# A wait for the landing behind each slot's four gathers in two layers of a graph network

## The reference

```
# layer 1 (graph attention, 4 heads)          # layer 3 (typed attention, 8 heads)
e = leaky_relu(a_s[src] + a_d[dst], 0.2)      attn = sum(Q[dst] * K[src]) * rel_scale[rel] / sqrt(16)
m = segment_max(e, dst)                       attn = attn - max(attn)
p = exp(e - m[dst])                           attn_exp = exp(attn)
z = segment_sum(p, dst)                       attn_sum = segment_sum(attn_exp, dst)
out = segment_sum(h[src]*p/z[dst], dst)       out = segment_sum(attn_exp/attn_sum[dst] * V[src], dst)
```

## Time and profile before

| | |
|---|---|
| time, median of 3 runs | 11803.96 us (11802.01 to 11812.33) |
| the profiled execution, its own time | 11689.37 us |
| its span | 11687.6 us |
| TensorE (PE) busy with matmuls / with weight loads | 6719.7 us (57%) / 5717.7 us (49%) |
| VectorE (DVE) busy | 4983.8 us (43%) |
| ScalarE (ACT) busy | 1831.9 us (16%) |
| GpSimd (POOL) busy | 6138.8 us (53%) |
| DMA over the span | 878.74 MB, mean 75 GB/s |

### The profile page before, as it was taken

How to read it: one execution, slowest core, us unless ns; L and a number is a source line. 1 busy time by engine, 2 the same in 40 slices (tenths; PEclk the granted TensorE clock), 3 DMA queues, 4 the chain that set the end, 5 groups by cost and what they waited for, 6 DMA issues and landing times. The chain is left out here.

```text
span 11687.6 us, 97629 instructions
## 1 busy us (share of the span) xinstructions
PE 6719.7 (57%) x31067; PEld 5717.7 (49%) x31067; DVE 4983.8 (43%) x11243; ACT 1831.9 (16%) x3088; POOL 6138.8 (53%) x6479
## 2 busy tenths in 40 slices
PE   4555555555436666666544545545543677777775
PEld 4444444444336666666534444444432455555553
DVE  4444444444552222222345555555555344444444
ACT  0000000000110000000110000000011454444543
POOL 4554555544216666666445555555530566666663
PEclk6666666666655555555566666666655677777776
DMA  4222222222112222222134343334320222222221
GB/s 133 73 76 75 76 76 73 76 76 76 36 28 55 55 56 54 55 55 55 50 122 122 120 124 120 122 120 122 122 68 1 65 63 61 61 61 61 63 61 38
DMA packets 388341, 878.74 MB, mean 75 GB/s; under 512 B 134341, under 2 KB 202872, under 8 KB 368224
## 3 DMA queue, kind: packets, MB, share of 16 engines
q0 software_dynamic: 232704, 536.56, 18.1%
q1 hardware_dynamic: 150242, 324.95, 8.5%
q10 hardware_dynamic: 4896, 11.01, 0.2%
HBM read 839.65 MB, written 32.40 MB: 75 GB/s over the span
## 5 line engine op out<-in xcount | busy, mean ns | idle before, releaser
L619 POOL DMA_INDIRECT PM<-gat_table,src_idx x1616 | 1525.6, 944 | 1532.7 <-PE ps L658 1023.2
L2074 POOL DMA_INDIRECT TMP<-schnet_table,src_idx x1616 | 1558.2, 964 | 1336.9 <-DVEq L2176 481.6
L1588 POOL DMA_INDIRECT PM<-hgt_kv_table,src_idx x1616 | 1527.7, 945 | 1356.8 <-PE ps L1620 743.2
L1148 POOL DMA_INDIRECT TMP<-gcn_table,src_idx x1616 | 1524.9, 944 | 1166.1 <-issue 452.9
L1166 PE MATMUL ps<-rows,PM 16*128 16x8 f32 x3232 | 756.1, 359 | 772.2 <-DVE PM L1213 755.3
L1166 PEld LDWEIGHTS ps<-rows,PM 16*128 16x128 f32 x3232 | 717.8, 323 | 871.5 <-DVE PM L1213 785.2
L1620 PE MATMUL ps<-PM 128*128 128x136 f32 x3232 | 628.0, 362 | 578.7 <-DVE PM L1709 577.6
L2101 PE MATMUL ps<-PM 128*128 128x128 f32 x3232 | 623.0, 355 | 488.9 <-issue 371.4
L1620 PEld LDWEIGHTS ps<-PM 128*128 128x128 f32 x3232 | 578.9, 261 | 612.7 <-DVE PM L1695 602.3
L1173 PE MATMUL ps<-TMP 128*128 128x128 f32 x3232 | 838.4, 441 | 0.2 <-DVE TMP L1207 0.2
L2101 PEld LDWEIGHTS ps<-PM 128*128 128x128 f32 x3232 | 572.1, 266 | 521.8 <-issue 521.4
(11 more groups left out here) (370 smaller groups left out, 9510.2 us busy)
## 6 DMA issues: line engine op xcount, KB each, us to landing
PM<-local_dst_row SPq DMA_DIRECT2D x101, 1024.0 KB
PM<-local_dst_row SPq DMA_DIRECT2D x202, 512.0 KB
PM<-in_attrT SPq DMA_DIRECT2D x101, 400.0 KB
PM<-gat_table,src_idx POOLq DMA_INDIRECT x1616
TMP<-gcn_table,src_idx POOLq DMA_INDIRECT x1616
PM<-hgt_kv_table,src_idx POOLq DMA_INDIRECT x1616
TMP<-schnet_table,src_idx POOLq DMA_INDIRECT x1616
xT<-in_rel_row SPq DMA_DIRECT2D x101, 128.0 KB
```

The lines of the kernel that those rows point to most:

```text
L619: pool.indirect_dma_start(out=g[:, par, t, 0:ROW0], out_offset=None, in_=tab0_d, in_offset=bass.IndirectOffsetOnAxis(ap=src_idx[:, i * ROU ...
L1148: pool.indirect_dma_start(out=g[:, b, k, :], out_offset=None, in_=tab1_d, in_offset=bass.IndirectOffsetOnAxis(ap=src_idx[:, (i * SLOTS + b ...
L1588: pool.indirect_dma_start(out=g[:, par, t, 0:2 * P], out_offset=None, in_=kv_d, in_offset=bass.IndirectOffsetOnAxis(ap=src_idx[:, i * ROUN ...
L2074: pool.indirect_dma_start(out=g[:, b, k, :], out_offset=None, in_=tab3_d, in_offset=bass.IndirectOffsetOnAxis(ap=src_idx[:, (i * SLOTS + b ...
```

## The change

One line is added in each of the two gather programs, behind the four gathers of a slot: GpSimd waits until that slot's gathers have all landed, and then goes on to the next slot. `g_ready[par][b]` is the semaphore that the gathers raise and that ScalarE (layer 1) and VectorE (layer 3) wait for as well; each gather adds 16, and slot `b` of half `par` is filled for the (j + 1)th time, so the value waited for is `16 * KT * (j + 1)`. The waits make 404 in each layer. All other instructions and their order on each engine stay as they were.

```
@@ layer 1 @@
                             t = b * KT + k
                             pool.indirect_dma_start(out=g[:, par, t, 0:ROW0], out_offset=None, in_=tab0_d,
                                                     in_offset=bass.IndirectOffsetOnAxis(ap=src_idx[:, i * ROUND + t:i * ROUND + t + 1], axis=0)).then_inc(g_ready[par][b], 16)
+                        pool.wait_ge(g_ready[par][b], 16 * KT * (j + 1))
                 straight(round_)
```

## The result

The change makes the kernel slightly slower: 11834.63 us (median of 11 runs, 11822.67 to 11848.08) against 11801.03 us before (11 runs, 11784.31 to 11813.63); ratio 1.0026, 95% interval 1.0018 to 1.0034. Forecast were 11464 us. The profiled execution has a span of 11832.9 us, 145 more than the one of before. The profile of before is of an execution of 11689 us, though, and the change was timed beside executions of 11801, so the differences between the two profiles need not add up to the difference of the times.

What follows compares the result with a forecast made beforehand. Bound: the VectorE/TensorE chain, delayed by TensorE completions seen late during gather bursts. Rounds of 29.9 and 27.1 us becoming 26.7 and 26.9 save 320 + 20 = 340 us: 11804 - 340 = 11464 us, range 11150 to 11830.

Steps and rivals of the forecast that it cites:

- The mechanism: Layers 1 and 3: rests behind each slot clear the gather backlog, so TensorE's completions come at once and GpSimd bounds.
- The chains: VectorE and TensorE steps of a round, claimed to need 19.7 us (layer 1) and 16.0 us (layer 3) without the delay.
- hold: TensorE's completions seen late by the waiting engine during gather bursts; put at 10.2 us a round (layer 1), 11.1 (layer 3).
- The second rival: Pauses too short: TensorE's completions stay held, bursts grow 4.4 us a round, 12684 us; slower outcomes had chance 0.20.
- the slots alone: Four slots a round, each 6.45 us including 2.45 for the landing: 25.8 us a round.
- the loads: SyncE's 1 MB a round falling beside an awaited gather: 0.9 us a round in layer 1, 1.1 in layer 3.
- one landing: Time from a slot's last gather start until its bytes are there and noticed: taken as 2.45 us.
- The prediction's sign for rests of 1.8 us with rounds over 28: What the changed profile would show if the VectorE and TensorE chains were longer than read.
- Only the third and fourth gather of a slot can pass their delay on: Reason for taking 0.9 us a round, from 0 to 3.7, for layer 1's load meeting a gather.
- The first rival: Layers cancel: shared DMA engines cost 2.7 us a round, rounds 28.5, layer 1 gains 140, layer 3 loses 140; chance 0.09.
- cost range of 24.8 to 31.8 us: Bounds of a round of four slots under the waits: landing seen with its bytes, or only when TensorE's completions are.
- The estimate worked out from "Anatomy of one DMA": About 2.0 us fixed plus bytes over 436 GB/s: a 70 KB gather lands in 2.2 us, a round takes 24.8.

Runs made afterwards that it cites:

- small_loads: The changed kernel, both waits kept, with SyncE's loads cut to 16 numbers a partition: 11402.27 us, ratio 0.9758 to the kernel before.
- the fourth set: Runs in which the kernel before took 9293.34 us; the change, run again there, took 11134.02 us, ratio 1.1987.
- pace_128: Kernel before plus GpSimd zeroing 128 numbers a partition behind each gather, no landing wait: ratio 0.9165 with the hold, 1.0711 without.
- pace_192: Kernel before plus GpSimd zeroing 192 numbers a partition behind each gather, no landing wait: 10811.37 us, ratio 0.9264.
- rest_long: Kernel before plus GpSimd zeroing a 128 x 512 scratch behind each slot's four gathers, no landing wait: 10990.79 us, ratio 0.9292.
- rest_640: Kernel before plus GpSimd zeroing 640 numbers a partition behind each slot, no landing wait: 10868.88 us, ratio 0.9295.

## Why the prediction was wrong

- **The mechanism held.** TensorE's completions come at once when GpSimd rests 1.8 us behind each slot, L807 and L816 lose their waits, and GpSimd becomes the bound. The chains fit under it with room: without hold and waits they fit under rounds of 20.0 us. The second rival (completions stay held, 12684) is refuted.
- **The step that failed is the size of a round under the waits.** Forecast were 26.7 and 26.9 us, measured 28.0 and 30.0, and with 29.8 and 27.1 before that turns a gain of 320 + 20 into a gain of 183 and a loss of 297 by the two profiles. By its terms (small_loads): the slots alone were put at 25.8 and take 26.4 and 27.9; the loads were put at 0.9 and 1.1 and cost 1.6 and 2.1. In layer 1 each term is short by 0.6 to 0.7 us, in layer 3 by 2.1 and 1.0. The largest error is that one landing, read off at 544 B a row in layer 1, was carried over to layer 3 at 1024 B. There, with small loads, two rests are 0.2 us longer than in layer 1, one 0.3 and one 0.9 (medians); the cause of the 0.9 stays open. The prediction's sign for rests of 1.8 us with rounds over 28 was longer chains, and it would have misled: the rounds are long because one or two rests in four are longer than 1.8 to 2.0.
- **"Only the third and fourth gather of a slot can pass their delay on"** was the argument for a small load term. It takes the meeting for chance. In the trace the load is issued during the same slot in 99 of 101 rounds of layer 1, and in layer 3 one of its halves during the first slot's last gather in 99 of 101, since by the code its cue (the four one-hot matrices) hangs on the chain that starts with a slot's landing. The trace of before could have said so: there the load of layer 1 comes behind a burst's last gather in 99 of 101 rounds. The first rival assumed the meeting and had the right sign for layer 3, but rounds of 28.5 in both layers, where 28.0 and 30.0 were measured; that its total of 11804 comes within 31 us of the result is luck.
- **The sum of the two layers** was the weak point of the whole: a large gain and a small one of opposite risk. Layer 3 had 0.2 us a round of forecast gain and a cost range of 24.8 to 31.8 us; a chance of loss there stood nowhere by itself.
- **The base of the sum** was mixed: rounds were read from an execution of 11689 us and their difference taken off a median of 11804. With the measured rounds the same sum gives 11804 - 183 + 297 = 11918, and 11834.63 was measured; so taking the rounds and the base from executions of two kinds would have put the sum off by some 80 us even with every round right.
- **The Trainium skill**, "DMA: Bandwidth & Descriptors", "Rules for kernel authors", says to issue early and wait late. The rule's sign was right for layer 3 and for the fourth set, and wrong for layer 1 where the hold exists, which gained 183 us. The estimate worked out from "Anatomy of one DMA" (24.8 us a round) was lower than mine and further off: the rows of small_loads give 26.4 and 27.9.
- **What no step had** is that the hold is not always there. Every figure of the earlier trace rows came from one execution; in the fourth set, where the hold is absent, the change costs 19.9%. The range, whose upper end of 11830 stood 5 us under the result, allowed for none of this.

## What to carry to other kernels

A wait added to a producer's queue makes a rhythm, and whatever other transfer takes its cue from that rhythm meets it at the same place every time: price such a meeting in full, and read the landing from the layer with the widest rows. When an engine's completion is seen late while GpSimd issues indirect gathers back to back, a rest helps, and the shortest one that works should be tried first: one wait a round or a short pause gave 7%, the wait behind each slot lost it again. Before tuning against a delay that no instruction accounts for, time the kernel again at another time and on other chips, because the cure may cost a fifth where the delay isn't. And take the profile of before from an execution like those that the change is timed against.

## What the runs showed of the hardware

- The same kernel took 9293 us in one set and 11672 to 11837 us in the others. The difference is in the layers that gather: a round of 16 indirect gathers of 128 rows takes 20.1 us where there is no hold, which is GpSimd's 1.25 us each, and 22.9 to 23.2 us where there is one (layer 2). The record has the number 13 for the chip both where before took 11672 and where it took 9293. So whether the hold belongs to a chip, to a machine or to something that was different at the time, no run shows, nor what it is that holds TensorE's completions.
- In the sets with the hold it fades with the spacing of gathers: at 1.25 us it costs layer 1 about 10 us a round (29.8 against 20.0), at 1.41 and 1.455 some 2.2 and 1.1 (24.7 against 22.5, 24.4 against 23.3), at 1.51 next to none (1.9 us of waiting for sums in the whole layer, in another set than the last two).
- The best kernels where the hold exists are pace_128 and pace_192 (ratios 0.9165 and 0.9264, each to the before of its own set), with rest_long and rest_640 close behind (0.9292, 0.9295). Where it doesn't exist no kernel that was measured beats the one before, and pace_128 is 7.1% behind it.
- A gather issued while another queue's load to all partitions is under way lands later: the rest after it was 3.6 us in the median in place of 1.9 (layer 1, a load of 1 MB against the shrunk one), and 3.9 and 3.1 in place of 2.8 and 2.2 (layer 3, loads of 512 KB).
